# Cross attention: four heads' scores side by side, both turns behind them

## The reference

```python
q = proj(x, Wq, bq); k = proj(ctx, Wk, bk); v = proj(ctx, Wv, bv)      # 16 heads of 16 columns
scores = einsum('bhqd,bhkd->bhqk', q, k) / sqrt(16)                    # 100 x 361 per head
p = softmax(scores, axis=-1)
x = einsum('bhqk,bhkd->bhqd', p, v)
return einsum('bsd,ed->bse', x, Wo) + bo                               # then layernorm(x + ...)
```

## Time and profile before

| | |
|---|---|
| median of 3 runs | 2338.49 us (2338.36 to 2340.51) |
| profiled execution | 2342.73 us, of which the span of the trace is 2341.1 us |
| PE, DVE, ACT, POOL busy | 2062.2, 1312.6, 1121.2, 516.1 us |
| scores of the cross attention (L968), first and last start | 495.1 and 878.6 us |
| 600 to 700 us: PE, DVE, ACT busy | 96.32, 55.23, 55.91 us |
| granted TensorE clock there | 1.00 |

### The profile page before, as it was taken

One profiled execution on the slowest core, in us unless ns is written; L12 is line 12 of the kernel. 1 busy time (PEld: TensorE's weight loads), 2 busy tenths in 40 slices (PEclk: granted clock), 3 DMA queues, 4 the chain that ended last, 5 costly groups with the idle time before them and its releaser, 6 DMA issues. The chain is left out here.

```text
span 2341.1 us, 48582 instructions
## 1 busy us (share of the span) xinstructions
PE 2062.2 (88%) x17426; PEld 1283.4 (55%) x17427; DVE 1312.6 (56%) x3201; ACT 1121.2 (48%) x2443; POOL 516.1 (22%) x599
## 2 busy tenths in 40 slices
PE   4888888789999996799989999999999999964993
PEld 2555555546666664566545555555555555552762
DVE  4788888535555553477835555555555555541224
ACT  2777776525555551277724444544444444420110
POOL 5677677111010001266510000000000000003002
PEclk8999999769999996899989999999999999977996
DMA  5000000022110000000000000000000000044102
GB/s 167 2 2 0 0 0 2 2 70 73 68 45 24 13 7 1 1 1 0 1 13 7 7 7 6 6 6 6 6 6 12 7 6 1 1 165 169 33 29 66
DMA packets 50376, 60.85 MB, mean 26 GB/s; under 512 B 9761, under 2 KB 44886, under 8 KB 49830
## 3 DMA queue, kind: packets, MB, share of 16 engines
q1 hardware_dynamic: 47278, 53.74, 7.4%
q0 software_dynamic: 3008, 5.91, 0.8%
HBM read 51.11 MB, written 8.52 MB: 25 GB/s over the span
## 5 line engine op out<-in xcount | busy, mean ns | idle before, releaser
L2367 ACT COPY la_pT<-la_pPT 128x400 f32<-128x400 f32 x246 | 122.0, 496 | 258.0 <-PE la_pPT L2120 257.5
L2089 PE MATMUL la_side<-la_wkv,la_inT 128*128 128x512 f32 (+1 forms) x512 | 243.9, 599 | 0.0
L2077 PE MATMUL la_side<-la_inT,la_wkv 128*128 128x461 f32 x512 | 225.5, 564 | 0.9 <-ACT la_inT L2342 0.8
L2257 DVE CUSTOM_DVE_ANT_0 la_pr<-la_pS,la_mb 100x461 f32<-100x461 f32 x256 | 148.2, 636 | 130.0 <-PE la_pS L2107 130.0
L2431 POOL TENSOR_TENSOR la_xb<-io_X,la_bo 100x256 f32<-100x256 f32 x16 | 11.7, 730 | 784.2 <-DVE io_X L2246 784.2
L2358 ACT ACTIVATE la_pr<-la_pr,la_nm 100x461 f32<-100x461 f32 x256 | 172.5, 681 | 0.0
L2120 PEld LDWEIGHTS la_pPT<-io_ident,la_pr 100*128 100x128 f32 x984 | 110.5, 142 | 102.3 <-issue 97.4
L1081 DVE TENSOR_REDUCE ca_nm<-ca_pS 100x2 f32<-100x722 f32 x128 | 116.2, 908 | 90.0 <-PE ca_pS L968 88.2
L2219 DVE COPY la_v<-la_side 128x512 f32<-128x512 f32 (+1 forms) x128 | 88.3, 690 | 131.0 <-PE la_side L2089 129.6
L1153 ACT ACTIVATE ca_pr<-ca_pS,ca_nm 100x361 f32<-100x361 f32 x256 | 130.0, 561 | 64.7 <-DVE ca_nm L1081 62.8
L2120 PE MATMUL la_pPT<-io_ident,la_pr 100*128 100x100 f32 x984 | 125.9, 250 | 1.1 <-issue 1.1
(11 more groups left out here) (360 smaller groups left out, 4256.6 us busy)
## 6 DMA issues: line engine op xcount, KB each, us to landing
rf_w<-in_L_ffn_W SPq DMA_DIRECT2D x16, 1024.0 KB
ca_cn<-in_ctx SPq DMA_DIRECT2D x16, 256.0 KB
far_cn<-in_ctx SPq DMA_DIRECT2D x16, 256.0 KB
rows_in<-io_zero SPq DMA_DIRECT2D x20, 128.0 KB, 1.8
rb_xr<-rows_in POOLq DMA_DIRECT2D x20, 128.0 KB, 2.3
rows_out<-rb_yr SPq DMA_DIRECT2D x20, 128.0 KB, 1.7
ea_wcT<-in_t_L_ffn_conv_W SPq DMA_DIRECT2D x1, 2048.0 KB
la_wkv<-in_L_xattn_Wkv SPq DMA_DIRECT2D x1, 2048.0 KB
```

The source lines that it names most:

```text
L2077: last = nc.tensor.matmul(pf[:, 0:SK], wkv[:, k, e * P:(e + 1) * P], inT[:, k, :], start=k == 0, stop=k == KD - 1)
L2089: last = nc.tensor.matmul(pf[0:keys[c], :], inT[:, k, c * P:c * P + keys[c]], wkv[:, k, o:o + 512], start=k == 0, stop=k == KD - 1)
L2257: ins = nc.vector.tensor_tensor_reduce(out=pr[m % 4][:, e, 0:SK], in0=pS[0:T, 2 * (m % 2) + e, 0:SK], in1=mb[b][:, :], scale=-1.0, scalar= ...
L2367: nc.scalar.copy(pT[m % 2][:, e, :], src[:, 0:NC * T]).then_inc(s_PT, 1)
```

## The change

A batch's 8 slots become 4 slots of two pairs (MQ = 4); slot j takes the side steps of the old slots 2j and 2j+1. On PE a slot is now: scores of both pairs, one after the other, with one wait that all earlier exps are done; turn of the first pair of the slot before; a side step; turn of its second pair; two side steps; values; a side step. On DVE: both maxima, a side step, the evac of the first turned pair, the rest. On ACT: a side step, exps of the first pair, a side step, exps of the second, the evac of the second turned pair, the rest; `sums` stands at the head of slot 2, `rstd` and `normed` in slot 3.

```diff
@@ PE, scores @@
-                    above(pe, s_P, n - 1)
+                    if m % 2 == 0:
+                        above(pe, s_P, n)
@@ PE, body @@
-                    for m in range(MP):
-                        n, small = i * MP + m, side.steps(i, m)
+                    for j in range(MQ):
+                        m, n = 2 * j, i * MP + 2 * j
+                        small = side.steps(i, m) + side.steps(i, m + 1)
...
                         scores(i, b, m)
-                        between()
-                        if m >= 2 or not first:
+                        scores(i, b, m + 1)
+                        if j or not first:
                             turn(n - 2, (m - 2) % MP)
                         between()
-                        if m >= 5 and m % 2:
-                            values(n - 4, i, b, m - 4)
-                        elif m % 2 and not first:
-                            values(n - 4, i - 1, 1 - b, MP - 4 + m)
+                        if j or not first:
+                            turn(n - 1, (m - 1) % MP)
+                        between()
+                        between()
+                        if j > 1:
+                            values(n - 3, i, b, m - 3)
+                        elif not first:
+                            values(n - 3, i - 1, 1 - b, MP - 3 + m)
+                        between()
@@ DVE, body @@
                         maxima(i, m)
-                        small = side.steps(i, m)
+                        maxima(i, m + 1)
+                        small = side.steps(i, m) + side.steps(i, m + 1)
                         for name, k in small[:1]:
                             step(name, k, i + 1 if name[0] == "f" else i - 1, 1 - b)
-                        if m % 2 == 0 and (m or not first):
-                            evac(n - 2, i * MQ + m // 2 - 1, (m - 2) % MP)
+                        if j or not first:
+                            evac(n - 2, i * MQ + j - 1, (m - 2) % MP)
                         for name, k in small[1:]:
                             step(name, k, i + 1 if name[0] == "f" else i - 1, 1 - b)
@@ ACT, body @@
+                        if j == 2 and not first:
+                            sums(i - 1)
                         for name, k in small[:1]:
                             step(name, k, i + 1 if name[0] == "f" else i - 1, 1 - b)
...
                         exps(i, m)
-                        if m % 2 and (m >= 3 or not first):
-                            evac(n - 2, i * MQ + (m - 1) // 2 - 1, (m - 2) % MP)
-                        if m == MP - 1 and not first:
+                        for name, k in small[1:2]:
+                            step(name, k, i + 1 if name[0] == "f" else i - 1, 1 - b)
+                        exps(i, m + 1)
+                        if j or not first:
+                            evac(n - 1, i * MQ + j - 1, (m - 1) % MP)
+                        if j == MQ - 1 and not first:
                             rstd(i - 1)
-                        for name, k in small[1:]:
+                        for name, k in small[2:]:
                             step(name, k, i + 1 if name[0] == "f" else i - 1, 1 - b)
```

More of the change, by code:

```diff
@@ L1091, in body @@
                     first = isinstance(i, int) and i == 0
-                    for m in range(MP):
-                        n = i * MP + m
+                    for j in range(MQ):
+                        m, n = 2 * j, i * MP + 2 * j
                         maxima(i, m)
-                        small = side.steps(i, m)
+                        maxima(i, m + 1)
+                        small = side.steps(i, m) + side.steps(i, m + 1)
                         for name, k in small[:1]:
                             step(name, k, i + 1 if name[0] == "f" else i - 1, 1 - b)
-                        if m % 2 == 0 and (m or not first):
-                            evac(n - 2, i * MQ + m // 2 - 1, (m - 2) % MP)
+                        if j or not first:
+                            evac(n - 2, i * MQ + j - 1, (m - 2) % MP)
                         for name, k in small[1:]:
                             step(name, k, i + 1 if name[0] == "f" else i - 1, 1 - b)
-                        if m == MP - 1 and not first:
+                        if j == MQ - 1 and not first:
                             normed(i - 1)
@@ L1168, in body @@
                     first = isinstance(i, int) and i == 0
-                    for m in range(MP):
-                        n = i * MP + m
-                        small = side.steps(i, m)
+                    for j in range(MQ):
+                        m, n = 2 * j, i * MP + 2 * j
+                        small = side.steps(i, m) + side.steps(i, m + 1)
+                        if j == 2 and not first:
+                            sums(i - 1)
                         for name, k in small[:1]:
                             step(name, k, i + 1 if name[0] == "f" else i - 1, 1 - b)
-                        if m == 4 and not first:
-                            sums(i - 1)
                         exps(i, m)
-                        if m % 2 and (m >= 3 or not first):
-                            evac(n - 2, i * MQ + (m - 1) // 2 - 1, (m - 2) % MP)
-                        if m == MP - 1 and not first:
+                        for name, k in small[1:2]:
[3 more added lines that the diff above has]
+                            evac(n - 1, i * MQ + j - 1, (m - 1) % MP)
+                        if j == MQ - 1 and not first:
                             rstd(i - 1)
-                        for name, k in small[1:]:
+                        for name, k in small[2:]:
                             step(name, k, i + 1 if name[0] == "f" else i - 1, 1 - b)
```

## The result

| | before | after |
|---|---|---|
| median | 2339.50 us (4 runs) | 2462.47 us (2459.66 to 2471.03, 4 runs) |
| ratio | 1 | 1.053, 95% interval 1.051 to 1.056 |
| span of the profiled execution | 2341.1 us | 2469.4 us |
| a full batch of cross attention | 24.19 us | 33.37 us |
| granted clock, 520 to 860 us | 1.00 | 0.84 |

The kernel is slower by 123 us, where 88 were forecast; the time lies 6 us above the forecast range. The direction and the place are as forecast. The batch is read from the starts of the scores: the second batch's first scores begin at 520.68, the last batch's at 987.80, (987.80 - 520.68)/14 = 33.37 us. 14 x (33.37 - 24.19) = 128.5 us, as much as the 128.3 us by which the span grew. The stage's first and last batch add 2.9 us, and what lies outside the stage took some 3 less.

The account below looks back on a forecast made before the run. PE's own instruction order was taken to bound the stage, at 96% busy. Waits of 80 us, edges of 3 and clock of 5 made 88; 2342.7 + 88, less 4.2, gave 2426 us, range 2404 to 2456.

Parts of the forecast that it names:

- Four heads on four strips: PE's scores in cross attention: 0.82 us for four heads, so 2.96 us of PE work go per batch.
- The waits: Second turns wait for DVE's late copy, next scores for exps in slot 1: batch 29.86 against 24.19 us, +5.7.
- The term of 80 us: Cross attention's 14 full batches, each 5.7 us longer by the laid-out slots: 14 x 5.7 = 80 us.
- The edges: First batch without backs and last without fronts: cost between nothing and 11 us, taken as 3 us.
- The clock: PE idles in slots 0 and 3 and its clock may fall: 5 us taken, bounds none and 24 us.
- One per batch: Upper bound on clock falls in the stage: one in each of 14 batches, 14 x 1.7 = 24 us.
- 1.7 us: Most PE work one clock fall makes late, from a trace where some 3.4 us ran at 1.2 GHz.
- near none: Clock cost in the stage taken as 5 us, since idle gaps are shorter than the busy work around them.
- the second rival: The waits as laid out, plus a clock that falls at least once in a batch: 2445 us, chance 15%.
- The one on the other side: Every wait covered, PE's work alone decides and 47 us go: faster, 2291 us, chance 4%.
- Half hidden: Waits half hidden because ACT or DVE gets ahead: 43 us more, 2381 us, chance 7%.
- nothing changes: Gain and loss cancel and the kernel stays at 2338 us, chance 2%.

Follow-up runs that it names:

- e2_copy_early: The changed kernel with DVE's copy of the first turned pair moved between the two maxima, ahead of the side step: 2388.0 us.
- e7_read_early: The kernel of e6_slot0 with DVE reading the first side step ahead of the second maximum: 2341.4 us.
- e6_slot0: Changed kernel with copy early, exps ahead of the second side step's read, values ahead of the third side step, slot 0 rearranged on PE and ACT: 2330.8 us.

## Why the prediction was right in part, and wrong in size

**Four heads on four strips: right.** 0.82 us per four heads were laid out, 0.80 is measured. What the packing gives was put at 2.96 us a batch; undone in a tight order it costs 3.41, of which some 0.6 is the wait that undoes it.

**The waits: right.** The chain in slot 3 (timeline of the changed kernel) is the one laid out: both maxima, by's reads, the copy, the turn. The scores ahead of it ran at 1.2 GHz; what sets the chain from 744.06 on is DVE's work, and from the first maximum to the turn it takes 3.58 us, where 3.65 were laid out.

```profile
744.06 1.73 DVE L1088 TENSOR_REDUCE ca_nm<-ca_pS 100x2 f32<-100x722 f32 x2 [3.32 <-PE ca_pS L969]
...
745.70 0.41 DVE L1072 TENSOR_TENSOR ca_y<-ca_side,ca_xb 100x256 f32<-100x256 f32 x1
...
746.15 0.43 DVE L1074 BATCH_NORM_STATS2 ca_stats<-ca_y 100x6 f32<-100x256 f32 x1
...
746.72 0.78 DVE L1095 COPY ca_pT<-ca_pPT 128x600 f32<-128x600 f32 x1
...
747.64 1.23 PE L978 MATMUL ca_pPT<-io_ident,ca_pr 100*128 100x100 f32 x6 [2.01 <-DVE ca_pT L1095]
```

The slots were forecast at 8.08, 7.21, 6.92 and 7.65 us, and measured at full clock at 8.01, 6.97, 6.78 and 7.53: 29.3 against 29.9. The term of 80 us measured 14 x 5.15 = 72. The edges, 3 us forecast: the last layer norm of the stage moved from 895.5 to 1025.4 and that of the stage ahead from 472.0 to 470.5, so the stage grew by 131.4 us, 2.9 more than 128.5. Two slips in the recorded sums changed little: 3.31 + 0.15 is 3.46 and not 3.44, and the upper end of the range counts the edges' 3 us twice, 2445 + 11 - 3 = 2453 and not 2456.

**The clock: the term that was mis-sized.** It was put at 5 us, with 24 as its upper bound; it measured 55. The waits came out at 70 instead of 83 us, which hid some of that: 50 too little and 13 too much make up the 35 us that were missed, to within 2 us. Three steps of that paragraph were wrong. "One per batch" as the bound on the number of falls had no row behind it: the batch shown has three, and a clock of 0.84 is some 32% of the time at 1.2 GHz, 11 us a batch (0.84 = 1 - x/2, x = 0.32). "1.7 us" for a fall was right for one of 3.4 us, but one of those shown lasts 7. And "near none, because the gaps are shorter than the work around them" ran against the rows it stood on. In the kernel before, the gap ahead of the fall of the earlier trace rows is 1.75 us, behind 12 us of unbroken work:

```profile
950.03 0.30 PE L1410 MATMUL ea_pt<-io_ident,ea_hn 100*128 100x100 f32 x1 [1.75 <-DVE ea_hn L1501]
```

What was right is the mechanism, and that it would be seen as a clock under 0.9. The Trainium skill's rule, in "TensorE: Matmul & The Clock Gate", section "A second HAM failure mode: psum-queue depth-cycling", that small idle gaps between groups of matmuls make the clock swing, agrees with the runs: 0.84 in the changed kernel, 1.00 with the gaps filled, nothing else moved. It should have carried the second rival to the front, and with more than one fall a batch. The kernel before had one short gap in each batch too, 0.6 to 0.8 us ahead of fc1, at a clock of 1.00; the changed one has seven or eight, of 0.3 to 2.1 us.

**The rivals.** The one on the other side, that PE's shorter work alone decides, is refuted for this order; but with a few steps moved in the queues the same four-head slots came to 2330.8, and to 2323.8 with the clock held, so the change's idea was sound and its order on DVE and ACT was not. Its end of 2291 us was not reached: the 23.17 us batch stands against 24.19 - 2.96 = 21.23. "Half hidden" and "nothing changes" are refuted by the slots.

## What to carry to other kernels

When an engine's work is packed tighter, look first at what stands in the other engines' queues ahead of the buffer it needs next: here one copy that stood behind two maxima instead of between them cost 74 us, some 45 of them as waits and the rest by the clock. Price idle gaps on TensorE twice, once as waiting and once as the half speed that follows; in a chain of several short gaps the second was nearly as large as the first (55 and 70 us). An order can be better at full clock and still lose, as 23.2 us a batch did against 24.0; idle matmuls in its waits show which of the two one is looking at.

## What the runs showed of the hardware

I had not expected gaps of 0.3 to 2.1 us, at most two or three in a slot, to hold TensorE at 1.2 GHz for a third of the time, nor that filling only the longest of them would change so little (0.84 to 0.87). Idle transposes, at most 24 in a slot and never read, raised the granted clock to 1.00 and took 55 us off the kernel. In e2_copy_early no gap is over 1.2 us and the clock is 0.89 all the same; in e7_read_early the same three gaps came before a fall in one batch and before none in another. Which pattern of gaps lets the clock fall, and why slots 0 and 1 of e7_read_early do and those of e6_slot0 don't, stays open. The gap ahead of the second turn of slot 0 is 0.63 us in the one and 0.38 in the other, but no run changed that gap alone.
